# Zeroing the masked probabilities by a minimum on VectorE instead of a select on GpSimd, with another opening, other buffers and another order in the last stage

## What is computed

```python
h = _layernorm(x) * (1 + ca) + sa
c_kv = h @ W_kv_down                       # 512 -> 128; k, v from c_kv, 16 heads of 32
scores = (q @ k^T + q_rope @ k_rope^T) / 8 # the rotary part, 32 wide, is shared by the heads
w = softmax(where(causal, scores, -inf))
x = x + ga * ((w @ v) @ W_o)
h = _layernorm(x) * (1 + cb) + sb
xr, xk = mu_r*h + (1-mu_r)*h_prev, mu_k*h + (1-mu_k)*h_prev   # h_prev: one token earlier
x = x + gb * (sigmoid(xr @ W_r) * (square(relu(xk @ W_k)) @ W_v))
```

## Time and profile before

| | |
|---|---|
| median of 3 runs (lowest, highest) | 3795.58 us (3789.31, 3804.19) |
| the profiled execution, its time | 3801.18 us |
| its span, first to last instruction | 3799.4 us |
| attention | 496.8 to 2907.3 us |
| last stage, from the block's start to the first r matmul | 2915.7 to 2970.9 us |
| last stage, the 15 chunks in the loop, then the last | 782.7 us, 45.8 us |
| granted clock of PE, mean | 0.969 |

### The profile page before, as it was taken

One profiled execution on the slowest core, in us unless ns is written; L12 is line 12 of the kernel. 1 busy time (PEld: TensorE's weight loads), 2 busy tenths in 40 slices (PEclk: granted clock), 3 DMA queues, 4 the chain that ended last, 5 costly groups with the idle time before them and its releaser, 6 DMA issues. The chain is left out here.

```text
span 3799.4 us, 55720 instructions
## 1 busy us (share of the span) xinstructions
PE 3586.7 (94%) x19296; PEld 2423.5 (64%) x19296; DVE 2702.1 (71%) x5390; ACT 1800.5 (47%) x3401; POOL 2722.6 (72%) x1225
## 2 busy tenths in 40 slices
PE   7999979999999999999999999999996899999998
PEld 4777746666666666666666666666663677777776
DVE  5676667777777777777777777777761777777775
ACT  2433325555555555555555555555553333333332
POOL 1333248889889898898898898988986455555555
PEclk8999989999999999999999999999997899999999
DMA  5789753463553544634635635445322111111110
GB/s 182 249 274 301 258 135 79 104 143 76 112 128 78 128 102 100 131 81 106 133 78 107 140 76 119 109 95 128 81 46 98 53 54 66 66 56 66 55 55 33
DMA packets 232263, 425.77 MB, mean 112 GB/s; under 512 B 25332, under 2 KB 26868, under 8 KB 231928
## 3 DMA queue, kind: packets, MB, share of 16 engines
q1 hardware_dynamic: 231992, 423.10, 43.0%
q10 hardware_dynamic: 64, 0.02, 0.0%
HBM read 300.86 MB, written 121.65 MB: 111 GB/s over the span
## 5 line engine op out<-in xcount | busy, mean ns | idle before, releaser
L853 ACT ACTIVATE att_probs<-att_ps_s 128x512 f32<-128x512 f32 (+3 forms) x2560 | 1311.8, 536 | 1014.6 <-PE att_ps_s L1006 915.1
L957 POOL TENSOR_TENSOR att_sum_g<-att_sum_g,att_probs 128x2048 f32<-128x2048 f32 (+3 forms) x432 | 1665.5, 3855 | 57.3 <-ACT att_probs L853 6.9
L888 DVE TENSOR_REDUCE att_piece_max<-att_ps_m 128x1 f32<-128x512 f32 x1536 | 970.8, 683 | 281.1 <-PE att_ps_m L991 278.8
L1005 PE MATMUL att_ps_s<-att_q_a,att_k_a 128*128 128x512 f32 (+3 forms) x2560 | 959.6, 379 | 13.3 <-DMA att_q_b<-att_neg_max 9.2
L1006 PE MATMUL att_ps_s<-att_q_b,att_k_b 65*128 65x512 f32 (+3 forms) x2560 | 932.2, 368 | 0.0
L891 DVE CUSTOM_DVE_ANT_0 att_ps_m<-att_ps_m,mask_qk 128x128 f32<-128x128 f32 (+3 forms) x1024 | 487.4, 512 | 292.5 <-PE att_ps_m L991 276.6
L991 PE MATMUL att_ps_m<-att_k_a,att_q_a 128*128 128x512 f32 (+3 forms) x1840 | 663.3, 383 | 17.1 <-PEq L215 13.7
L1005 PEld LDWEIGHTS att_ps_s<-att_q_a,att_k_a 128*128 128x128 f32 x2560 | 486.4, 190 | 195.1 <-issue 91.1
L1012 PE MATMUL att_ps_o<-att_probs,att_v 128*32 128x512 f32 (+3 forms) x5120 | 561.3, 546 | 32.7 <-POOL att_probs L929 32.7
L1006 PEld LDWEIGHTS att_ps_s<-att_q_b,att_k_b 65*128 65x128 f32 x2560 | 485.7, 190 | 61.2
L991 PEld LDWEIGHTS att_ps_m<-att_k_a,att_q_a 128*128 128x128 f32 x1840 | 348.5, 191 | 235.8 <-issue 105.1
(11 more groups left out here) (173 smaller groups left out, 5096.8 us busy)
## 6 DMA issues: line engine op xcount, KB each, us to landing
att_q_a<-s_q_hi SPq DMA_DIRECT2D x128, 256.0 KB, 6.0
att_q_a<-s_qr_hi SPq DMA_DIRECT2D x128, 256.0 KB, 7.1
prj_x_sb<-in_x_dram SPq DMA_DIRECT2D x16, 1024.0 KB, 5.3
s_q_hi<-prj_q_hi SPq DMA_DIRECT2D x16, 1024.0 KB, 4.4
s_q_lo<-prj_q_lo SPq DMA_DIRECT2D x16, 1024.0 KB, 6.5
s_k_hi<-prj_k_hi SPq DMA_DIRECT2D x16, 1024.0 KB, 4.5
s_k_lo<-prj_k_lo SPq DMA_DIRECT2D x16, 1024.0 KB, 6.5
s_v<-prj_v_sb SPq DMA_DIRECT2D x16, 1024.0 KB, 9.3
```

What stands on the lines that cost most here:

```text
L853: act.activation(probs[t % RING][:, hh, c0:CH], ps_s[(GH * t + hh) % SBANKS][:, c0:CH], ACT.Exp, scale=SCALE).then_inc(probs_ready, 1)
L888: dve.tensor_reduce(top, ps_m[:, bank, :], AX_X, ALU.max).then_inc(piece_taken, 1)
L957: pool.tensor_tensor(sum_g[:, :, c0:CH], sum_g[:, :, c0:CH], new, ALU.add).then_inc(sum_added, 1)
L1005: mm(out[:, c0:CH], k_a[:, hh, i * P:(i + 1) * P], q_a[j][:, hh, c0:CH], start=True, stop=False)
```

## The change

In attention:
- The zeroing moves to DVE: a table `past` (128x128, made once by POOL: 1e30 where the key is not after the query, 0 elsewhere), and `min(probs, past)` in place on the triangle of the four heads, one `tensor_tensor` of 128x512 in each diagonal step. It stands in `extras[t + 1]` for step t. POOL's adds of diagonal steps wait for it.
- `SHARE_OF`: steps 20 (chunk 2, i = 8) and 30 (chunk 3, i = 6) go from PE's ones-matmul to POOL's adds.
- `deal` counts each minimum as `CLEARING` = 5 units of DVE's work.
- During the last unit SP loads the four raw weights and the first chunk's attention rows for the last stage, into memory of their own.

In the last stage:
- The four weight buffers are no longer parts of working tiles; several big tiles take over memory of attention's operands.
- Opening: high and low parts of w_o and of the attention rows are made block by block in turn; the gates are loaded per batch entry, the first one first; the output projection of chunk 0 stands half before and half after the second transpose.
- Modulation goes from DVE to ACT (`Identity` with scale and bias). The mixes are written to PSUM (`ps_t`) instead of SBUF and read there by ACT and by DVE's low part. ACT's casts of k's mix alternate with the sigmoids. DVE's product of values and gate goes to buffers of the key stage (`gated`), and the wait for `y_ready` moves from the sigmoids to the first two key steps.

The core of the diff:

```diff
-SHARE_OF = ("GGTT", "GGGGGGGG", "GGGGGGGGTGGG", "GGGGGGTGGGGGTGGG")
+SHARE_OF = ("GGTT", "GGGGGGGG", "GGGGGGGGGGGG", "GGGGGGGGGGGGTGGG")
...
-PIECE, CLOSING = 2.8, 19
+PIECE, CLOSING, CLEARING = 2.8, 19, 5
...
-    closes = lambda m: CLOSING * any(FIRST[j] + 2 == 2 * m for j in range(TCH))
+    cleared = lambda s: any(0 <= s - 1 - FIRST[j] - TB * j < TB for j in range(TCH))
+    closes = lambda m: CLOSING * any(FIRST[j] + 2 == 2 * m for j in range(TCH)) + CLEARING * sum(map(cleared, (2 * m, 2 * m + 1)))
...
+            def load_for_last_stage(j):
+                wait_alone(sp, scores_ready, GH * (NSTEP * (NU - 1) + FIRST[j] + STEPS[j]), sp_mark)
+                if j == 0:
+                    wait_alone(sp, o_stored, 16 * (TCH * (NU - 2)), sp_mark)
+                    sp.dma_start(ops["raw"]["att"][:], scratch["o"].rearrange("(g n) p t -> n p g t", g=NG)[0]).then_inc(ops["att_in"], 16)
+                    load_weight(0)
+                    load_weight(3)
+                else:
+                    load_weight(j)
...
+            def clear_future(u, j, i):
+
+                at = probs[(FIRST[j] + i) % RING][:, :, (i - TB * j) * P:(i - TB * j + 1) * P]
+                dve.wait_ge(probs_ready, heads_ready(u, FIRST[j] + i, GH - 1))
+                dve.tensor_tensor(at, at, past[:][:, None, :].broadcast_to([P, GH, P]), ALU.min).then_inc(cleared, 1)
...
+            for t, (u, j, i) in enumerate(STEP_OF):
+                if i >= TB * j:
+                    extras[t + 1].append(lambda u=u, j=j, i=i: clear_future(u, j, i))
...
-            def clear_future(u, j, i):
-
-                at = probs[(FIRST[j] + i) % RING][:, :, (i - TB * j) * P:(i - TB * j + 1) * P]
-                pool.affine_select(out=at, in_=at, compare_op=ALU.is_ge, fill=0.0, base=0, pattern=[[0, GH], [1, P]],
-                                   channel_multiplier=-1).then_inc(cleared, 1)
+            pool.wait_ge(ones_ready, 1)
+            pool.memset(past[:], -MASKED).then_inc(past_ready, 1)
+            pool.wait_ge(past_ready, 1)
+            pool.affine_select(out=past[:], in_=past[:], compare_op=ALU.is_ge, fill=0.0, base=0, pattern=[[1, P]],
+                               channel_multiplier=-1).then_inc(past_ready, 1)
...
+                if i >= TB * j:
+                    pool.wait_ge(cleared, future_cleared(u, j, i))
+                else:
+                    pool.wait_ge(probs_ready, heads_ready(u, s, GH - 1))
...
-        x_sb = sb("x_sb", [P, TB, D], F32)
+        x_sb = ops["v"].rearrange("p a b c -> p (a b c)").rearrange("p (m d) -> p m d", m=TB)
...
-        mix_f = sb("mix_f", [P, 2, 2, CH], F32)
-        mix_r, mix_k = pair("mix_r", [P, NC, CH]), pair("mix_k", [P, NC, CH])
+        mix_r, mix_k = (ops["q_a"][0], ops["q_a"][1]), (ops["q_a"][2], ops["q_b"][0])
...
-            def modulate(n, c):
-                dve.wait_ge(t_ready, NC * n + c + 1)
-                dve.tensor_scalar(h2[:, c, 1:1 + CH], ps_t[:, c, :], keep["mod"][:, 3, c, bass.ds(n, 1)],
-                                  keep["mod"][:, 2, c, bass.ds(n, 1)], ALU.mult, ALU.add).then_inc(h2_ready, 1)
...
-                dve.scalar_tensor_tensor(out=mix_f[:, c % 2, j, :], in0=diff[:, c, :], scalar=mu[:, j, c:c + 1],
+                dve.scalar_tensor_tensor(out=ps_t[:, 2 * j + c % 2, :], in0=diff[:, c, :], scalar=mu[:, j, c:c + 1],
                                          in1=h2[:, c, 0:CH], op0=ALU.mult, op1=ALU.add).then_inc(mix_ready[j], 1)
...
-                dve.tensor_tensor(gate_r[:, m, :], ps[:, m, :], gate_r[:, m, :], ALU.mult).then_inc(taken[m], 1)
+                dve.tensor_tensor(gated[m], ps[:, m, :], gate_r[:, m, :], ALU.mult).then_inc(taken[m], 1)
...
+            def modulate(n):
+                act.wait_ge(carry_ready, n + 2)
+                for c in range(NC):
+                    act.wait_ge(t_ready, NC * n + c + 1)
+                    act.activation(h2[:, c, 1:1 + CH], ps_t[:, c, :], ACT.Identity, scale=keep["mod"][:, 3, c, bass.ds(n, 1)],
+                                   bias=keep["mod"][:, 2, c, bass.ds(n, 1)]).then_inc(h2_ready, 1)
...
-                for m in range(TB):
-                    act.wait_ge(*ready(f"r{m}", n))
-                    act.wait_ge(y_ready, TB * n + 1)
-                    act.activation(gate_r[:, m, :], ps[:, m, :], ACT.Sigmoid).then_inc(taken[m], 1)
+                for c in range(NC):
+                    mix_high(n, 1, c)
+                    if c:
+                        gate(n, c - 1)
+                gate(n, TB - 1)
...
             act.wait_ge(w_in[0], 16)
-            act.copy(w_o[0][:], w_raw[0][:]).then_inc(w_hi, 1)
-            split_attention(0)
+            act.wait_ge(att_in, 16)
+            for g in range(NG):
+                act.copy(att[0][:, g, :], first_att[:, g, :]).then_inc(att_hi, 1)
+                act.copy(w_o[0][:, g, :], w_raw[0][:, g, :]).then_inc(wo_hi, 1)
...
+            turn_weight(1)
+            attention_out(0, False, range(0, 2))
+            turn_weight(2)
+            attention_out(0, False, range(2, TB))
+            turn_weight(3)
```

More of the change, by code:

```diff
@@ L959, in _ @@
+                    mine = [n for n, o in enumerate(SHARE_OF[j]) if o == "G"]
+                    for i in mine[1:]:
+                        add(u, j, i, mine)
             for u in range(NU):
@@ L1063, in _, with feedforward @@
                     close_denominators(*closing)
[L1066 removed]
+def feedforward(nc, keep, dram, scratch, out, ops):
     with ExitStack() as ctx:
@@ L1317, in split_attention, with gate, mix_high @@
                     act.copy(att[0][:, g, :], att_f[:, g, :]).then_inc(att_hi, 1)
-            def mix_high(n, j):
+            def modulate(n):
[4 more added lines that the diff above has]
+                                   bias=keep["mod"][:, 2, c, bass.ds(n, 1)]).then_inc(h2_ready, 1)
+            def gate(n, m):
+                act.wait_ge(*ready(f"r{m}", n))
+                act.activation(gate_r[:, m, :], ps[:, m, :], ACT.Sigmoid).then_inc(taken[m], 1)
+            def mix_high(n, j, *part):
                 dst = (mix_r, mix_k)[j]
-                for c in range(NC):
+                for c in part or range(NC):
                     act.wait_ge(mix_ready[j], NC * n + c + 1)
-                    act.copy(dst[0][:, c, :], mix_f[:, c % 2, j, :]).then_inc(mix_hi[j], 1)
+                    act.copy(dst[0][:, c, :], ps_t[:, 2 * j + c % 2, :]).then_inc(mix_hi[j], 1)
             def keep_x1(n):
```

171 lines of the change are left out of this document (97 added, 74 removed).

## The result

The changed kernel takes 3969.12 us (median of 4 runs, 3963.47 to 3972.08) where the kernel before takes 3792.44 (3788.59 to 3804.19) beside it: ratio 1.0459, 95% interval 1.0431 to 1.0487. The forecast was 3838 and the range ended at 3900. The sign was right, the size was not: +44 us was forecast, +177 measured.

The account below looks back on a forecast made before the run. The prediction took TensorE as the bound in attention, with GpSimd close. Attention +148, chunks -88 and opening -16 sum to +44 us: 3801.2 + 44 = 3845, on the runs' scale some 3838; range 3685 to 3900.

Parts of the forecast that it names:

- four legs: Attention unit, cut by the starts of GpSimd's sums: 10.85, 30.09, 45.60 and 62.19 us before; the last engine decides each.
- The minimum: Attention, VectorE: each minimum waits for the end of GpSimd's running add; mean 2.2 us or more, ending 0.55 after it.
- Rival A: Attention: the minimum doesn't wait for a long add and costs 0.7 us; time 3684; chance 0.25.
- The sum of the legs: Attention unit after the change: 13.2 + 31.9 + 48.2 + 64.5 = 157.8 us, 9.1 more than 148.7.
- rival B: Attention: three more TensorE stops a unit each cost 1.7 us at half clock, +5 a unit; time 3913; chance 0.12.
- Two sums leave PE: Attention: 32 groups of eight ones-matmuls go, 32 us less for TensorE, counted only where TensorE is last.
- Last unit: Attention's last unit: no pieces to deal after step 24, GpSimd bounds it, +11 us.
- Chunks: Last stage, 15 chunks: 52.2 us each becomes 46.3, -88 us in all, bounds -50 and -95.
- the alternating order: Last stage, ScalarE: sigmoids alternate with key casts, against TensorE's 3.27 us wait a chunk for the sigmoid.
- Opening: Last stage's start to first receive matmul, 55.2 us: loads hidden in the last unit, -16 us, bounds -8 and -22.
- adds beside minima: Sign in attention: GpSimd's adds after a minimum last 4.85 us.
- TensorE's idle share: Sign in attention: TensorE's idle time before maxima and closes goes from 2% to some 8% of a unit.

Follow-up runs that it names:

- minima at nothing: The changed kernel with each minimum cut to one column and one input, future keys no longer zeroed: 3740.21 us, ratio 0.9844.
- the sums alone: The changed kernel with the zeroing back on GpSimd and CLEARING 0, keeping the two more sums on GpSimd: 3803.09 us, ratio 1.0030.
- the filled kernel: The changed kernel with 36 repeated score matmuls a unit just ahead of TensorE's four stops: 3866.58 us, ratio 1.0199.

## Why the prediction was right and wrong

- **What bounds attention** was read rightly: four legs, GpSimd late in the second already and in the third by little. The minimum was priced at 2.2 us in the mean and is 2.10 over all 256 (2.13 in the steady units), those shown ending 0.55 us after an add. Rival A (0.7 us) is out, and so was its time: with minima at nothing the kernel takes 3740, not 3684. A's fourth leg was put at 61.7 and is 64.9, and one more add in GpSimd's chain is what the two kernels share: with the sums alone that leg is 64.5.
- **The sum of the legs** was 157.8. Without half clock (the filled kernel) it is 159.7, with it 167.1. The terms that were mis-sized by themselves are the second leg (31.9 against 33.0) and the fourth (64.5 against 66.2); the first and third were put 0.7 and 0.3 too high, which in part hides it.
- **The step that failed is the clock.** The forecast's legs hold TensorE's work at full clock and put the half clock behind its stops at nothing; rival B priced it, at 1.7 us lost for each of three more stops, +5 a unit. At half speed 1.7 us are lost in 3.4 us, so B has some 10 us a unit at half clock. Measured are 23 us a unit at half clock, 5.8 for each of the four stops, and 7.4 us lost: in the two windows above it lasted 5.4 us behind the stop of 2.89 and 6.7 us behind that of 1.84. And the reason given against B, "where POOL is last a slower PE costs nothing", failed in the third leg: GpSimd was last up to 46.30, as forecast, but behind it the close needs TensorE, which stood at half clock just then and took 3.89 us for the 1.51 of the filled kernel. That the minima alone would do it is not so either: with the old shares they leave the clock at 1.00, and the two sums alone bring it to 0.95. The 14 steady units are 14 x 9.3 = 130 us over the forecast; 14 x 7.4 = 104 of them are this.
- **Not weighed:** that CLEARING = 5 is a wrong price. By the plan's own units (2.8 for a piece of 0.60 us) a minimum of 2.1 us is 9.8. The prediction worked the plan through with 5 and didn't ask whether it fits; with 12 the kernel is 106 us faster.
- **Two sums leave PE.** Counted at nothing where TensorE isn't last, which held: nothing is gained, the sums alone cost 7.2 us a unit, part of it by half clock, which the prediction did not look for there.
- **Last unit:** 167.0 for 152.0, +15, forecast +11. The first unit: 187.5 for 179.5, +8 where 9.1 was taken.
- **Chunks:** -87.5 for -88. The terms that carried it were right in size (VectorE's turns with GpSimd, the modulation off its chain, the clock from 0.96 to 0.99), and one was given to the wrong edit, the alternating order.
- **Opening:** from TensorE's last close in attention (ends at 2908.35 before, 3192.87 after) to the first receive matmul 62.6 us before and 40.7 after, -21.9 for -16, just inside the bound of -22. VectorE's memset and four low parts took 1.77 + 5.70 = 7.5 us for the 8.6 assumed, and TensorE started on the first of them. The last chunk is 4.2 us shorter (41.6 for 45.8), which the sum had not counted.
- **The account:** attention +283.1, opening -21.9, chunks -87.5, last chunk -4.2, the first stage +1.4: +170.9, and the difference of the spans is 171.0, 3970.4 - 3799.4. The forecast had +148, -16 and -88.
- **Signs that didn't come:** adds beside minima were to last 4.85 us and last 4.56 to 4.59 (the next one just starts later); TensorE's idle share was to be 8% and is 6.4%, VectorE's busy share 90% and is 84.6%, both of a longer unit.
